# The fp4 feed-forward stage: half of a scaling product and a whole rescaling product move from VectorE to GpSimd

## The reference

```python
def fp4_quant_dequant(x):
    xb = x.reshape(shape[:-1] + (shape[-1] // BLOCK, BLOCK))      # BLOCK = 16
    scale = jnp.max(jnp.abs(xb), axis=-1, keepdims=True) / 6.0
    scale = jnp.maximum(scale, jnp.float32(1e-12))
    xn = xb / scale
    idx = jnp.searchsorted(_MID, jnp.abs(xn))
    q = _GRID[idx] * jnp.sign(xn) * scale
    return q.reshape(shape)

def fp4_linear(x, w):
    xq = fp4_quant_dequant(x)
    wq = fp4_quant_dequant(w)
    return jnp.einsum('bsk,nk->bsn', xq, wq)
```

## Time and profile before

| | us |
|---|---|
| median of three runs | 5982.3 |
| lowest and highest | 5974.27, 5985.24 |
| the profiled execution, device time | 5974.55 |
| its span in the profile | 5972.8 |
| VectorE busy in the span | 4178.2 (70%) |
| TensorE busy in the span | 5509.4 (92%) |
| GpSimd busy in the span | 2257.3 (38%) |

### The profile page before, as it was taken

How to read it: one execution, slowest core, us unless ns; L and a number is a source line. 1 busy time by engine, 2 the same in 40 slices (tenths; PEclk the granted TensorE clock), 3 DMA queues, 4 the chain that set the end, 5 groups by cost and what they waited for, 6 DMA issues and landing times. The chain is left out here.

```text
span 5972.8 us, 119449 instructions
## 1 busy us (share of the span) xinstructions
PE 5509.4 (92%) x37453; PEld 3412.9 (57%) x37453; DVE 4178.2 (70%) x9588; ACT 2810.8 (47%) x4608; POOL 2257.3 (38%) x3170
## 2 busy tenths in 40 slices
PE   7997999999999899999999999999998879996787
PEld 5664444444444477647775677567764446644564
DVE  6785666666666688648874788478855866677864
ACT  4554222222222255545555455555555655544454
POOL 6662000000000366436653566356632532254322
PEclk9998999999999899999999999999998989998899
DMA  4333333333333565325551555155520000000002
GB/s 133 104 108 104 99 95 97 97 96 95 97 96 97 139 161 158 100 71 151 156 144 40 145 156 157 28 149 158 155 61 5 0 7 0 0 1 0 2 1 65
DMA packets 526333, 527.07 MB, mean 88 GB/s; under 512 B 55698, under 2 KB 436705, under 8 KB 503780
## 3 DMA queue, kind: packets, MB, share of 16 engines
q1 hardware_dynamic: 517684, 517.90, 31.6%
q10 hardware_dynamic: 8320, 5.25, 0.4%
HBM read 337.88 MB, written 185.07 MB: 88 GB/s over the span
## 5 line engine op out<-in xcount | busy, mean ns | idle before, releaser
L1195 DVE TENSOR_REDUCE a_mx<-a_unit 128x2 f32<-128x512 f32 (+1 forms) x1536 | 1033.7, 687 | 307.9 <-PE a_unit L1491 303.3
L1338 ACT ACTIVATE a_prob<-a_slot 128x1536 f32<-128x1536 f32 x512 | 743.3, 1452 | 551.0 <-PE a_slot L1514 466.1
L2179 ACT ACTIVATE f_silu<-f_pG 128x512 f32<-128x512 f32 x528 | 315.0, 598 | 932.9 <-PE f_pG L2263 918.9
L1489 PE MATMUL a_unit<-a_sk,a_sq 96*128 96x128 bf16 (+1 forms) x4096 | 597.4, 249 | 41.0 <-DMA a_sk<-a_kscratch 25.2
L2114 DVE TENSOR_TENSOR f_gated<-f_spread,f_silu 128x512 f32<-128x512 f32 x512 | 362.9, 709 | 339.8 <-ACT f_silu L2179 295.1
L60 POOL TENSOR_SCALAR f_veps<-f_moments 128x4 f32<-128x4 f32 (+1 forms) x112 | 26.3, 234 | 1413.8 <-DVE f_moments L1990 1018.4
L2231 PE MATMUL f_pO<-f_hidden,f_wd 128*128 128x512 f32 x1056 | 546.0, 599 | 13.6 <-DVE f_hidden L2116 12.9
L2263 PE MATMUL f_pG<-f_xnT,f_wg 128*128 128x512 f32 x1056 | 541.4, 594 | 0.0
L2267 PE MATMUL f_pU<-f_xnT,f_wu 128*128 128x512 f32 x1056 | 540.2, 593 | 0.0
L1491 PE MATMUL a_unit<-a_maskq,identb 128*128 128x256 bf16 (+1 forms) x1536 | 481.5, 313 | 2.1 <-issue 2.1
L1135 POOL TENSOR_SCALAR_AFFINE_SELECT a_prob<-a_prob 128x512 f32<-128x512 f32 x384 | 244.5, 637 | 520.2 <-ACT a_prob L1338 506.5
(11 more groups left out here) (476 smaller groups left out, 12148.6 us busy)
## 6 DMA issues: line engine op xcount, KB each, us to landing
f_spread<-f_scratch SPq DMA_DIRECT2D x1024, 128.0 KB, 2.9
a_sq<-a_qscratch SPq DMA_DIRECT2D x128, 768.0 KB, 5.6
a_sk<-a_kscratch SPq DMA_DIRECT2D x160, 384.0 KB, 6.5
a_qscratch<-a_parts SPq DMA_DIRECT2D x288, 192.0 KB, 2.2
a_qscratch<-a_parts SPq DMA_DIRECT2D x288, 128.0 KB, 2.2
a_kscratch<-a_parts SPq DMA_DIRECT2D x160, 192.0 KB, 2.2
a_kscratch<-a_parts SPq DMA_DIRECT2D x160, 128.0 KB, 2.2
a_qscratch<-a_parts SPq DMA_DIRECT2D x288, 64.0 KB, 1.8
```

The lines of the kernel that those rows point to most:

```text
L1195: v.tensor_reduce(dst, src, op=ALU.max, axis=AX.X, negate=True).then_inc(red_done, 1)
L1338: act.activation(prob[gr % 2][:, :], slot[:, :], ACT.Exp, scale=SCALE).then_inc(exp_done, 1)
L1489: pe.matmul(bank[:, at * wide:(at + 1) * wide], q, sk[b][0:KM, gr * GH + h, 0:wide], start=(at == 0), stop=False)
L2179: act.activation(silu[c % 2][:, :], pG[c % 2][:, :], ACT.Silu).then_inc(silu_done, 1)
```

## The change

GpSimd gets two products. The first is the second half (704 of 1408 columns) of `yh = hid * inv`. VectorE does the first half, behind a new increment of `inv_done` that GpSimd waits for. ScalarE's `absh` waits for both halves (`yh_done`, `late_done`), and VectorE waits for `late_done` before `product(2)` overwrites `hid`. The second is the whole of `xq = yx * nscx`, at the end of GpSimd's step, behind a new `rx_done`. The wait for `t_pe` goes with it, and VectorE waits for `xq_done` before it overwrites `nscx`.

```diff
+                    if is_block(n):
+                        o = 1 - b
+                        g.wait_ge(inv_done, n + 1)
+                        g.tensor_tensor(by16(yh[o][:, HALF:]), by16(flat(hid)[:, HALF:]), spread16(inv[:, HB:]),
+                                        op=ALU.mult).then_inc(late_done, 1)
                     if is_block(n + 2):
                         g.wait_ge(invx_done, n + 3)
...
                         g.tensor_tensor(shift[:, :], away[:, :], rstd[:, :], op=ALU.mult).then_inc(rstd_done, 1)
+                    if is_block(n + 2):
+                        g.wait_ge(rx_done, n + 3)
+                        if is_block(n + 1):
+                            g.wait_ge(t_pe, n + 2)
+                        g.tensor_tensor(by16(flat(xq)), by16(yx[:, :]), spread16(nscx[:, :]), op=ALU.mult
+                                        ).then_inc(xq_done, 1)
                 blocks_by_two(g, step)
...
-                        scaled(flat(hid), yh[b][:, :], nsch[b][:, :], WIDE).then_inc(yh_done, 1)
+                        link(inverse(flat(hid), nsch[b][:, :], inv[:, :], WIDE))
+                        v.sem_inc(inv_done, 1)
+                        v.tensor_tensor(by16(yh[b][:, 0:HALF]), by16(flat(hid)[:, 0:HALF]), spread16(inv[:, 0:HB]),
+                                        op=ALU.mult).then_inc(yh_done, 1)
                         v.drain()
                     if is_block(n + 2):
                         v.wait_ge(xn_done, n + 3)
+                        if is_block(n + 1):
+                            v.wait_ge(xq_done, n + 2)
                         inverse(flat(xn), nscx[:, :], invx[:, :], BLK).then_inc(invx_done, 1)
...
                         rounded(yx[:, :], absx[:, :])
-                        if is_block(n + 1):
-                            v.wait_ge(t_pe, n + 2)
-                        unscaled(flat(xq), yx[:, :], nscx[:, :], BLK).then_inc(xq_done, 1)
+                        v.sem_inc(rx_done, 1)
                     if is_block(n):
                         v.wait_ge(ah_done, n + 1)
                         rounded(yh[b][:, :], absh[:, :])
                         v.sem_inc(rh_done, 1)
+                        v.wait_ge(late_done, n + 1)
                     product(2)
...
                         act.wait_ge(yh_done, n + 1)
+                        act.wait_ge(late_done, n + 1)
                         act.activation(absh[:, :], yh[b][:, :], ACT.Abs, scale=TWO_BITS).then_inc(ah_done, 1)
```

More of the change, by code:

```diff
@@ L2855, in fp4_feed_forward @@
         (apart, stats_done, rstd_done, xn_done, yx_done, ax_done,
-         yh_done, ah_done, xq_done, invx_done, rh_done, t_pe, xqT_done, gu_pe, silu_done, hid_done, hq_done, h_pe, hT_done, o_pe, x_done) = k.sem(
+         yh_done, ah_done, xq_done, invx_done, inv_done, late_done, rx_done, rh_done, t_pe, xqT_done, gu_pe, silu_done, hid_done, hq_done, h_pe, hT_done, o_pe, x_done) = k.sem(
             "apart stats_done rstd_done xn_done yx_done ax_done "
-            "yh_done ah_done xq_done invx_done rh_done t_pe xqT_done gu_pe silu_done hid_done hq_done h_pe hT_done o_pe x_done")
+            "yh_done ah_done xq_done invx_done inv_done late_done rx_done rh_done t_pe xqT_done gu_pe silu_done hid_done hq_done h_pe hT_done o_pe x_done")
         by16 = lambda x: x.rearrange("p (b e) -> p b e", e=B16)
@@ L2908, in inverse @@
                     return v.reciprocal(to, to)
[L2910 to L2914, removed]
                 def rounded(y, magnitude):
@@ L2920, in rounded @@
                                                 op1=ALU.subtract))
-                def unscaled(dst, y, nsc, width):
-                    return v.tensor_tensor(by16(dst), by16(y), spread16(nsc), op=ALU.mult)
                 def step(i, j):
```

## The result

The changed kernel took 5999.06 us (median of 7 runs, 5990.61 to 6004.17), the kernel before 5977.71 beside it. The ratio is 1.0031 with a 95% interval of 1.0021 to 1.0042, so the change costs 13 to 25 us. I had forecast 5978.0 with 5986 as the upper end. The time is near that of rival B, 5995.6.

A forecast was written before the change was run, and what follows sets the result against it. VectorE's own queue sets the pace; 0.74 + 0.57 - 0.88 - 0.05 = 0.38 us a block, 5.3 for 14 blocks, less 1.0 at the end, saves 4.3: median 5978.0 us, 8 in 10 within 5963 to 5986.

The forecast's parts named there:

- rival B: Half product of yh: GpSimd also gets in first, VectorE's half waits 1.26 us in 14 blocks, total 5995.6; chance 0.10.
- The half product: Scaling product yh: VectorE saves 0.74 us a block and starts first by 0.07 or more, so GpSimd's half is blocked.
- the sign of a fault at this step: Block time in the changed kernel's timeline: over 16 us would make the forecast wrong at the half product.
- The product of the normed rows: Moving xq saves VectorE 0.57 us; GpSimd starts 0.05 before the second rounding of yh, costing 0.88 a block.
- Increments and waits: Increments and the two added waits cost 0.05 us a block, bounds 0 to 0.15.
- ScalarE's cover: GpSimd's half ends 2.2 us after the inverse; delayed absh is over at 3.6, before absx's yx at 4.0.
- Rivals A and C: Second rounding of yh: VectorE gets in first (A, 5966.7 us) or nothing blocks (C, 5965.6); chance 0.24 together.

The follow-up runs named there:

- e1: Changed kernel with GpSimd's half product waiting for the end of VectorE's half; stage 275.15 us, ratio to the kernel before 1.0007.
- e4: Changed kernel with one unused increment between GpSimd's wait and its half product; stage 273.52 us, ratio to the kernel before 1.0005.
- e2: Changed kernel with the scaling product whole on VectorE again, only xq on GpSimd; stage 278.76 us, ratio to the kernel before 1.0015.
- e10: Changed kernel with an unused increment ahead of the half, and an increment and three fills ahead of xq; stage 271.42 us, ratio to before 0.9996.
- e13: Changed kernel with an unused increment ahead of the half, xq released between VectorE's roundings of yh behind another increment; stage 278.56 us, ratio to before 1.0012.
- e9: Changed kernel with yh whole on VectorE and GpSimd's xq behind the second rounding of yh; stage 291.51 us, ratio to before 1.0024.
- e11: Changed kernel with xq back on VectorE and an unused increment ahead of GpSimd's half product; stage 268.37 us, ratio to before 0.9995.
- e8: Changed kernel with an unused increment ahead of the half and xq behind the second rounding of yh; stage 268.39 us, ratio to before 0.9999.

## Why the prediction was wrong, point by point

- **The half product (the step that failed).** "VectorE's half starts after 0.08 to 0.11. So VectorE is first by 0.07 or more." Both ends of this comparison were off. VectorE started 0.12 after the reciprocal (5555.86 to 5555.98), GpSimd 0.11 after it, not 0.18. The 0.18 had been read behind a rounding, and the 0.08 behind a reciprocal, and I compared a gap behind one instruction with a gap behind another. The right row was already there: after the second rounding and the increment of `rh_done`, GpSimd's `hq` starts at 5559.63 in the earlier trace rows, and VectorE's own next product starts at 5559.63 in the earlier trace rows. An increment behind a drain lets both go in the same hundredth. That is rival B's "its start and VectorE's draw level", which deserved far more than a chance of 0.10. Which of the two would win the tie couldn't be read from the rows (in the earlier trace rows it was VectorE). The runs showed GpSimd ahead by 0.01, VectorE's half at 2.12 for 0.89, and a block of 16.70, over the 16 that the prediction had named as the sign of a fault at this step.
- **Its price.** Rival B said 1.26 a block; 2.12 - 0.89 = 1.23 was measured, and 5978.0 + 14 x 1.23 = 5995.2. The measured median is 3.9 above that, inside the spread of the runs. Nearness to a microsecond is partly luck: the median of the kernel before, 5982.3 of three runs in the forecast, was 5977.71 of seven and, beside e1 to e4, 5983.02 of 31.
- **The product of the normed rows.** It went as forecast: `shift` 1.53 (about 1.5), the product 1.05 (1.06), 0.06 ahead of the rounding (0.05), the rounding 2.48 (2.5), so 0.85 for the 0.88. What leaves VectorE was worth 0.64 and not 0.57, since its roundings of `yx` and `yh` lie 0.12 apart (5563.48 to 5563.60) and not 0.18. e2 showed it alone. In block 13 it was the first rounding that was held up (2.53, the second 1.63), not the second.
- **Increments and waits.** 0.05 a block was low. The gap ahead of the reduction over `xn` grew from 0.16 to 0.25, that ahead of `hid` from 0.19 to 0.21, and the increment made 0.12 of 0.08: 0.15 together, the upper bound I had given. With 0.49 for the half (2.12 for 1.63), 0.85 and less 0.64 this makes 0.85 a block, as measured.
- **ScalarE's cover** held: the half was done on both engines 2.24 after the reciprocal (5558.10), as with the forecast 2.2, and VectorE waits for no `absh` or `absx` between 5440 and 5640. In the last two blocks 1.1 was lost for the forecast 1.0, and in the opening ones 0.8 gained, for which I had taken nothing.
- **What the forecast missed besides.** With the half product in VectorE's favour (e4) the block is 15.65, not 15.5, mainly through the waits and through `q_nscx`, 0.28 for 0.18. Rivals A and C, 14.6 a block with `xq` behind the rounding, overlooked the ring through TensorE. Such blocks exist (14.6 to 14.8 in e10 and e13), but where TensorE's clock fell behind the wait for `xq` they took 16.5 to 17.1 in e13 and e9.

The best stages, e11 and e8, are 6 us shorter than before's. No kernel here is measurably faster than the kernel before as a whole.

## What to carry to other kernels

Before work with two inputs in SBUF is given to GpSimd, put its start beside the start of VectorE's instruction at the same place, from one and the same row pair and not from gaps behind different instructions. At a tie take the loss as the likely case, and let VectorE go first by a margin of 0.1 us (one more increment in GpSimd's queue was enough at the half; at the other place an increment and a fill moved the start by less than 0.05). What is then saved on VectorE is lost again if it comes out of the slack of the operand that TensorE waits for.

## What the runs showed of the hardware that I had not expected

- The border of who goes first is sharp, wherever both starts could be read (at equal starts in the earlier trace rows it was VectorE that kept its length). GpSimd's start 0.06, 0.02 and 0.01 before VectorE's: VectorE blocked in every case (2.48, 2.52, 2.12). 0.09 to 0.13 after it: GpSimd blocked in every case (2.05, 2.42). Nothing was shared out between them.
- An increment behind a drain let the waiting GpSimd instruction start no later than VectorE's own next one (5555.97 and 5555.98).
- A GpSimd product blocked VectorE's one-input `TENSOR_SCALAR` on 32 columns (0.18 to 0.50 us), and left `TENSOR_REDUCE` on 512 columns alone (0.69 in both).
- The same hole of 2.34 us in TensorE's work was followed by a granted clock of 1.00 in one block and 0.50 in another of the same execution, the blocks differing by 1.7 us.
